# Chunked gated delta attention on one core: three pieces of the per-chunk preparation earlier in their engines' orders, three later

## The reference, cut to what matters

```python
xn = layernorm(layernorm(x)) * ln_w + ln_b        # two normalisations, one behind the other
q, k, v = xn @ Wq.T, xn @ Wk.T, xn @ Wv.T
alpha, aR = sigmoid(xn @ Wa.T + ba), sigmoid(xn @ WaR.T + baR)
beta, gamma = sigmoid(xn @ Wb.T + bb), sigmoid(xn @ Wg.T + bg)   # the gates, one number per head
def step(S, R):                                    # one token
    kn = k_t / norm(k_t)
    r = clip(v_t - S.T kn, -1, 1)                  # the clipped error of the state's prediction
    S = a_t * S;  S = S + b_t * kn * (v_t - S.T kn)
    R = aR_t * R; R = R + g_t * kn * (r - R.T kn)
    o = S.T q_t + R.T q_t
out = os @ Wo.T + residual
```

## Time and profile before

| | us |
|---|---|
| median of three runs | 3606.68 (3600.88 to 3606.81) |
| the profiled execution: its own time, its span | 3596.48, 3594.6 |
| DVE busy in the whole span | 2525.7 (70%) |
| PE busy in the whole span (matmuls) | 3199.4 (89%) |
| the stretch of the 32 chunks, about | 980 to 3110 |

### The profile page before, as it was taken

How to read it: one execution, slowest core, us unless ns; L and a number is a source line. 1 busy time by engine, 2 the same in 40 slices (tenths; PEclk the granted TensorE clock), 3 DMA queues, 4 the chain that set the end, 5 groups by cost and what they waited for, 6 DMA issues and landing times. The chain is left out here.

```text
span 3594.6 us, 144990 instructions
## 1 busy us (share of the span) xinstructions
PE 3199.4 (89%) x64390; PEld 2378.8 (66%) x64390; DVE 2525.7 (70%) x5676; ACT 1396.1 (39%) x3203; POOL 945.4 (26%) x1051
## 2 busy tenths in 40 slices
PE   6874999998699999999999999999999999758888
PEld 4654999987466666666666666666666666535555
DVE  6774111121688888888888888888888888729887
ACT  2221222221354554545555455455545545321111
POOL 2244122212222232223223323222332322211110
PEclk9886999999899999999999999999999999979999
DMA  2116666665000000000000000000000000010000
GB/s 66 47 61 204 185 184 191 187 207 175 23 9 10 8 11 9 9 10 9 10 8 11 10 8 11 8 10 8 11 10 8 11 8 8 5 48 17 24 24 14
DMA packets 98187, 168.37 MB, mean 47 GB/s; under 512 B 15400, under 2 KB 71976, under 8 KB 97312
## 3 DMA queue, kind: packets, MB, share of 16 engines
q1 hardware_dynamic: 76976, 136.07, 11.5%
q0 software_dynamic: 19440, 21.97, 4.3%
q10 hardware_dynamic: 1152, 1.06, 0.1%
HBM read 118.86 MB, written 38.09 MB: 44 GB/s over the span
## 5 line engine op out<-in xcount | busy, mean ns | idle before, releaser
L1067 POOL TENSOR_TENSOR da_M<-da_M,da_decay 128x512 f32<-128x512 f32 x256 | 261.3, 1046 | 790.4 <-DVE da_TT L1215 438.7
L1379 ACT COPY da_Ub<-da_U 32x256 f32<-32x256 f32 x1024 | 412.2, 403 | 17.2
L1210 DVE TENSOR_TENSOR da_eGn<-da_eGn,da_z 128x30 f32<-128x30 f32 (+14 forms) x960 | 328.2, 342 | 33.0
L1209 DVE TENSOR_TENSOR da_z<-da_eGn 128x30 f32<-128x30 f32 (+14 forms) x960 | 329.2, 343 | 27.6
L1671 PE MATMUL da_C<-da_Ub,da_Km 128*64 128x256 f32 x2048 | 294.6, 406 | 4.9 <-ACT da_Ub L1379 3.4
L1501 PE MATMUL da_unit<-early_buffer,da_xnT 128*128 128x512 f32 x512 | 284.9, 642 | 9.7 <-DVE da_sp L1151 6.4
L840 PEld LDWEIGHTS le_ps_qkv<-le_scr,le_up 128*128 128x128 f32 x2272 | 265.8, 193 | 4.8 <-ACT le_scr L670 1.8
L840 PE MATMUL le_ps_qkv<-le_scr,le_up 128*128 128x128 f32 x2272 | 267.8, 277 | 1.2 <-ACT le_scr L670 1.2
L1372 ACT COPY da_U<-da_A 128x256 f32<-128x256 f32 x256 | 95.4, 373 | 421.3 <-PE da_A L1642 421.2
L1509 PE MATMUL da_unit<-da_xnT,early_buffer 128*128 128x128 f32 x2048 | 242.2, 277 | 9.9 <-ACT da_eGn L1364 9.9
L1642 PEld LDWEIGHTS da_A<-da_W,da_TT 32*32 32x32 f32 x8192 | 127.5, 106 | 183.6 <-DVE da_W L1228 68.5
(11 more groups left out here) (299 smaller groups left out, 7014.3 us busy)
## 6 DMA issues: line engine op xcount, KB each, us to landing
le_up<-in_upT SPq DMA_DIRECT2D x71, 1024.0 KB, 5.0
le_scr<-moe_slots SPq DMA_DIRECT2D x71, 129.0 KB, 4.2
le_down<-in_downT SPq DMA_DIRECT2D x8, 1024.0 KB, 12.3
early_buffer<-in_x SPq DMA_DIRECT2D x16, 256.0 KB, 3.8
moe_acc<-le_y SPq DMA_DIRECT2D x32, 128.0 KB, 2.4
da_x<-moe_acc SPq DMA_DIRECT2D x128, 32.0 KB, 1.8
stream<-da_xz SPq DMA_DIRECT2D x128, 32.0 KB, 1.6
stream<-da_y POOLq DMA_DIRECT2D x128, 32.0 KB, 2.8
```

Source lines behind the costliest of these rows:

```text
L1067: ins = nc.gpsimd.tensor_tensor(st_, st_, decay[:, par, rec, 2 * g:2 * g + 2].rearrange("p a b -> p (a b)").unsqueeze(2).to_broadcast([P, ...
L1209: c.link(tt(t, Xm[:, s + 1:C, s:s + 1].to_broadcast([P, below, s]), Xm[:, s:s + 1, 0:s].to_broadcast([P, below, s]), ALU.mult))
L1210: c.link(tt(Xm[:, s + 1:C, 0:s], Xm[:, s + 1:C, 0:s], t, ALU.add))
L1379: ins = nc.scalar.copy(Ub[rows_of(b), :, :, b, :], U[rows_of(b), rec])
```

## The change

It moves instructions in the lists of POOL, DVE and PE; it adds and removes none. SP's and ACT's lists stay as they are. Ahead of the loop `residual(0)` and `norm_third(0)` are called right behind `norms(0)` and `norm_second(0)`, of which they were part.

```diff
 POOL
 def norms(n):
     need(pool, var_ready, n * 2 + 1)
     ... rstd[:, 0:1] ... .then_inc(rstd_ready, 1)
+    need(pool, var_ready, n * 2 + 2)
+    nc.gpsimd.tensor_tensor(rstd[:, 1:2], ve[:, 1:2], mhalf[:], ALU.pow).then_inc(rstd_ready, 1)
+
+def residual(n):
     need(pool, z_ready, n + 1)
     need(pool, xz_stored, n * (16 * B))
     nc.gpsimd.tensor_tensor(xz[:], x[:], z[:], ALU.add).then_inc(xz_ready, 1)
-    need(pool, var_ready, n * 2 + 2)
-    nc.gpsimd.tensor_tensor(rstd[:, 1:2], ve[:, 1:2], mhalf[:], ALU.pow).then_inc(rstd_ready, 1)
...
                 if prepare:
                     factors(i + 1, 1 - par)
+                if norm:
+                    residual(i + 2)
                 if state:
                     rescale(i, par, 3)
 DVE
 def norm_second(n):
     ... z ... .then_inc(z_ready, 1)
+
+def norm_third(n):
     need(dve, z_ready, n + 1)
     variance(1, z)
...
-def gates(n):
+def gates_in(n):
     need(dve, bg_psum, n + 1)
     tt(bg[:], un[:, 0, 0:2 * H], bbg[:], ALU.add).then_inc(bg_ready, 1)
+
+def gates_out(n):
     need(dve, bge_ready, n + 1)
     ... nsig ... .then_inc(sig_ready, 1)
...
 def period(i, par):
-                if state:
-                    state_rows(i, 0)
                 if norm:
                     norm_first(i + 2)
...
                 if prepare:
                     norms_of_keys(n)
+                    gates_in(n)
                 if state:
                     clipped(i, par, 0)
                     update(i, 0, 0)
                 if norm:
+                    norm_third(i + 2)
+                if prepare:
+                    gates_out(n)
+                if norm:
                     norm_last(i + 2)
                 if prepare:
-                    gates(n)
                     products(n, pn, 1, 1)
...
                     triangle_out(n)
+                    state_rows(n, 0)
                 if state:
                     update(i, 3, 1)
 PE
                 if put:
                     result(i - 1, 1)
+                if prepare:
+                    gram(n, pn, 1)
                 if state:
                     state_predicted(i, par, 2)
-                if prepare:
-                    gram(n, pn, 1)
                 if put:
                     result(i - 1, 2)
```

More of the change, by code:

```diff
@@ L1114, in _ @@
             norms(0)
+            residual(0)
             every_period(period)
@@ L1313, in _ @@
             norm_second(0)
+            norm_third(0)
             norm_last(0)
```

## The result

The changed kernel takes 3586.85 us (median of 7 runs, 3584.2 to 3594.61), the kernel before 3606.81 in the same runs (3599.82 to 3612.82). The ratio is 0.9949 [0.9935, 0.9963]: it is faster by 18.4 us, with 13.3 to 23.4 as the ends of the interval. The forecast was 46.8 us. The sign was right, the size was not, and 3586.85 lies 1.85 us above the range.

The account below looks back on a forecast made before the run. DVE's work ahead of the clipped errors and ACT's late copy were taken to bound the period; 54.6 + 13.4 - 2.36 n, with n = 9, gave 46.8 us, so 3606.7 becomes 3560, range 3537 to 3585.

Parts of the forecast that it names:

- What bounds T to X: Triangle's end to `turn_x`: DVE decides until the clipped errors, then PE, delayed by ACT's copy; 1.82 us per undisturbed period.
- DVE's and ACT's terms: Ahead of `turn_x`, per undisturbed period: 0.95 us from DVE's earlier clipped errors, 0.87 from ACT's earlier `da_U` copy.
- The clock: Behind the triangle, PE's low clock was to become rarer: 9 periods instead of 12, each taking 2.36 us off the gain.
- the formula: Gain in us over 30 periods: 68.0 - 2.36 n, where n counts the periods of low clock.
- The drops always sit in this place: Claim that the granted clock falls only in the 12 us behind the triangle, in 12 of 31 stretches before.
- the mechanism on the other side: Low clock behind the triangle in all 30 periods: gain -2.8 us, time 3609; above 26 periods had chance 0.03.
- POOL later ... I take zero: POOL's delayed work meets DVE's `products` once or twice per period, 0.55 us each, absorbed by DVE's idle time: zero cost.
- the rival: POOL's meetings with DVE's `products` come into the open: 16 us less gain, 3576 us; chance 0.08.
- xn waits for POOL: Ahead of `turn_x`, POOL's scaled values shut xn out: 0.5 us in 21 periods, 10.5 us less gain, 3570.5; chance 0.12.
- Gram ... I take zero: Gram of group 1 ahead of PE's predicted rows: DVE's fourth mask product 0.3 us earlier, counted zero, up to 2 us gain.
- Behind L1487 PE goes on as before: After `turn_x` PE's steps keep their distances and all that waits for PE moves with it, so the gain stays.

## Why the prediction was right and where it was wrong

**What bounds T to X, and DVE's and ACT's terms: right.** In the undisturbed periods the median of T to X fell by exactly the 1.82 us that the forecast worked out. L1236 is 0.43, ACT's wait 1.94, PE's first wait 0.53, and the wait for `da_U` is gone. The split is borne out as well: with the bias alone the median went from 11.26 to 10.38 (0.88, forecast 0.87 for ACT), and the rest of the change took it on to 9.44 (0.94, forecast 0.95 for DVE). The parts do not add up in any order, though: the variance without the bias lost 36.4 us.

**The clock: right in direction, and within its scatter.** Low periods went from 12 to 7, and to 11 in the repeat; I took 9. With that the formula gives 68.0 - 2.36 x 7 = 51.5 and 42.0, and T to X by the traces gave 48.6 and 40.5. "The drops always sit in this place" held before; in each trace of the changed kernel the clock also fell twice, for 3.4 us, some 32 to 35 us behind T. The case in which the clock falls in all periods, which I had as the mechanism on the other side with 0.03, did not come with this change, but one further edit on PE brought it: 28 of 30. What PE did ahead of the drop there was the norms, with wide matmuls in place of the small ones.

**"POOL later ... I take zero": the first step that failed.** The meetings with `products` came as foreseen, but neither their price nor the idle time that was to swallow them held. A product beside the decay lasts up to 1.53 us for 0.68, so 0.85 and not 0.55, and often two in a row do. And the 0.62 and 0.68 us of idle time in the earlier trace rows lie ahead of the products; between them and the clipped errors of group 1, whose end PE waits for, DVE has one wait, 0.42 in the period of the earlier trace rows and 0.72 on average, where the products became 0.86 longer on average and up to 2 us in a period. In some periods the decay met the clipped errors instead (L1235's 0.96 - 0.42 = 0.54). By the runs it cost 22 us (0.9937 against 0.9875) or 14 (0.9906 against 0.9945), where the rival had 16 at a chance of 0.08; in the kernel before the same late decay changed nothing (1.0001). What was missing is one list: for each moved instruction of POOL, what DVE does in the microseconds in which it lands, and how long DVE waits between that place and the next result that PE needs.

**xn waits for POOL: right as a mechanism, wrong as a price.** xn waits (0.19 by the profile, and its duration 0.69 for 0.40), and the rival's 0.12 was for 10.5 us. PE's weight load waits for it 14 times, 4.2 us in all, in the changed kernel, and taking the meeting away from the kernel with the late sum and decay changed nothing measurable. By the Trainium skill (SBUF — State Buffer, "Who interferes with whom") such a wait was to be expected for a fast `tensor_scalar`; the trace agrees with the wait, at 0.29 us.

**"Gram ... I take zero": the second step.** It costs 11 us in one pair (0.9906 against 0.9875) and 4, not clear of noise, in the other (0.9945 to 0.9949 against 0.9937), where I allowed up to 2 us of gain. My reason was that PE's work up to the predicted rows is unchanged. It is; but DVE's wait for them grew from 21.9 to 60.4 us (26.0 with the gram back, 30.2 with POOL late too), and PE's pauses are longer. From X to C they are 38.1 us against 25.8 in one pair and 41.9 against 32.8 in the other; that is 0.41 of the 0.58 us per period that X to C is longer, and 0.30 of 0.55. The rest, and why the order of two dense blocks lengthens the pauses, stay open.

**PE's own pauses: not in the sum at all.** This is the third step: "Behind L1487 PE goes on as before". I read PE's waits in two places of a timeline and took that for granted. PE's pauses were 42.4 us in the stretch before, and 63.8 after. What a wait of PE costs is partly given back by the blocks of instructions that arrive in it; take the wait away, and PE reaches the end of its blocks sooner: with POOL's instructions late, 15.2 us of waits for DVE went from X to C and 7.0 us of pauses came. That the number of instructions counts is shown by the price of the extra matmuls (1.9 us per us of small ones, 0.5 of wide ones) and by where the pauses end. Without the gram's move the traces have 49.1 - 42.4 = 6.7 us more pauses than before, and 56.6 - 42.4 = 14.2 with POOL's waits gone as well; each is one execution.

Together, from the ratios: with the gram back and POOL's sum and decay late, the kernel is 45.0 us faster than before, where the forecast was 46.8. That this is so close is partly luck, since 14 us more pauses are still in it and the first rows alone gave more than they were priced at.

## What to carry to other kernels

When an instruction of POOL is moved, its cost is where it lands: look at what DVE executes there and at DVE's idle time between that and the next result that another engine waits for. Idle time ahead of the meeting does not help. Add up the waits that no semaphore explains ahead of a forecast; where there are many and they stand at fixed numbers of instructions, time gained ahead of a stretch of many short matmuls can be partly given back, and an added short matmul costs more than its duration. But before short matmuls are replaced by wide ones, compare what they take and look at the granted clock behind them: here T to X became 1.9 us longer, more than the pauses had taken.

## What the runs showed of the hardware

- PE stopped for 0.15 (the least that the profile lists) to 2.4 us at a time, at near multiples of 254 to 256 of its listed instructions, 65 to 112 times in the stretch of the chunks (32.9 to 77.8 us). In all 14 traces it went on 2.1 to 3.1 us after a load of 16 KB began, and no two loads began less than 3.2 us apart.
- A DVE product of 512 elements with two inputs took 0.68 us, and up to 1.53 beside POOL's decay of a state.
- Sixteen wide matmuls in place of 64 small ones, of 1830 in a period, took the granted clock of the stage from 0.99 to 0.96 and cost 54 us. Eight of the wide ones took 0.96 us and 32 of the small ones 0.36, both at the full clock. What it was in that order that brought the clock down was not taken apart.
- A one-input DVE `tensor_scalar` of 256 elements, which has no shorter duration than a two-input instruction of that size (0.40 and 0.42 us), still waits for POOL: its median went from 404 to 693 ns. The power of POOL on 128x16 elements, 2.9 us long, held up none of the DVE instructions beside it that could be compared: a product beside it took 0.68 us as elsewhere.
